# Moving an aggregation and a spread of sums ahead of a product in a graph network's layers: one TensorE order, one VectorE order

## The reference

```python
for l in range(attn_w.shape[0]):                       # 3 layers
    si = x @ attn_w[l, :d]
    sj = x @ attn_w[l, d:]
    scores = si[:, :, None] + sj[:, None, :] + attn_b[l]
    scores = jnp.where(scores >= 0, scores, 0.2 * scores)
    scores = jnp.where(mask, scores, -jnp.inf)
    attn = jax.nn.softmax(scores, axis=-1)
    agg = jnp.einsum('bij,bjd->bid', attn, x)
    h = layernorm(x + agg, g1[l], beta1[l])
    ff = jax.nn.gelu(h @ W1[l] + b1[l], approximate=False) @ W2[l] + b2[l]
    x = layernorm(h + ff, g2[l], beta2[l])
```

## Time and profile before

| | |
|---|---|
| median of 3 runs | 1641.13 us (1639.92 to 1642.3) |
| the profiled execution, its own time | 1641.3 us |
| its span, first to last instruction | 1639.5 us |
| mean granted PE clock, share of full | 0.996 |
| busy share of the span: PE, PEld | 98%, 88% |
| busy share: DVE, ACT, POOL | 81%, 75%, 81% |

### The profile page before, as it was taken

One profiled execution on the slowest core, in us unless ns is written; L12 is line 12 of the kernel. 1 busy time (PEld: TensorE's weight loads), 2 busy tenths in 40 slices (PEclk: granted clock), 3 DMA queues, 4 the chain that ended last, 5 costly groups with the idle time before them and its releaser, 6 DMA issues.

```text
span 1639.5 us, 40121 instructions
## 1 busy us (share of the span) xinstructions
PE 1611.0 (98%) x12036; PEld 1435.8 (88%) x12036; DVE 1320.2 (81%) x5321; ACT 1232.7 (75%) x2856; POOL 1327.4 (81%) x2367
## 2 busy tenths in 40 slices
PE   9999999978999999999999999999999999999997
PEld 8888888867898999989899898989989899898986
DVE  5999999987777777787877777777787888888875
ACT  7888898866777676777767776677777778787874
POOL 7788888856677787877878777787878999999996
PEclk9999999999999999999999999999999999999999
DMA  6334322212122121212213121121211222222211
GB/s 229 104 104 140 101 91 91 90 40 91 40 101 91 50 77 38 77 50 66 77 40 102 64 77 63 52 77 39 77 42 61 77 77 77 77 90 85 82 47 57
DMA packets 141721, 127.62 MB, mean 78 GB/s; under 512 B 12240, under 2 KB 132560, under 8 KB 141648
## 3 DMA queue, kind: packets, MB, share of 16 engines
q1 hardware_dynamic: 141648, 126.81, 24.2%
HBM read 89.04 MB, written 37.75 MB: 77 GB/s over the span
## 4 chain that ended last, share of the span: by engine, by line
PE 75%; DVE 1%; POOL 1%; ACT 0%; issue 0%; POOLq 0%; DVEq 0%; ACTq 0%
PE ps L45 33%; PE ps L979 32%; PE ps L951 5%; PE ps L965 3%; PE ps L943 1%; PE ps L958 1%; POOL n L169 0%; DVE gnn_junk L1111 0%; DVE xo L1222 0%; DVE res L1154 0%; POOL gnn_inv_last L913 0%; ACT gnn_w_hi L1067 0%; DVE gnn_st L1225 0%; DVE gnn_st L1178 0%; DVE gnn_st L1159 0%
## 5 line engine op out<-in xcount | busy, mean ns | idle before, releaser
L979 PE MATMUL ps<-gnn_w_hi,gnn_g_hi 128*128 128x256 f32 x1536 | 434.0, 283 | 1.5 <-DVE gnn_res L1174 1.5
L979 PE MATMUL ps<-gnn_w_lo,gnn_g_hi 128*128 128x256 f32 x1536 | 429.0, 279 | 0.0
L979 PE MATMUL ps<-gnn_w_hi,gnn_g_lo 128*128 128x256 f32 x1536 | 428.7, 279 | 0.0
L1079 ACT ACTIVATE gnn_g_hi<-ps,b_cols 128x512 fp32r<-128x512 f32 x384 | 264.4, 688 | 199.3 <-PE ps L45 199.3
L1182 DVE TENSOR_TENSOR gnn_g_lo<-ps,gnn_g_hi 128x512 fp32r<-128x512 f32 x384 | 262.8, 684 | 103.5 <-ACT ps L1080 103.4
L45 PE MATMUL ps<-gnn_hT_hi,gnn_w_hi 128*128 128x512 f32 x768 | 337.9, 440 | 0.0
L45 PE MATMUL ps<-gnn_hT_lo,gnn_w_hi 128*128 128x512 f32 x768 | 303.6, 395 | 0.0
L45 PE MATMUL ps<-gnn_hT_hi,gnn_w_lo 128*128 128x512 f32 x768 | 303.5, 395 | 0.0
L979 PEld LDWEIGHTS ps<-gnn_w_hi,gnn_g_hi 128*128 128x128 f32 x1536 | 288.7, 188 | 3.9 <-DVE gnn_res L1174 1.7
L979 PEld LDWEIGHTS ps<-gnn_w_lo,gnn_g_hi 128*128 128x128 f32 x1536 | 288.8, 188 | 2.3
L979 PEld LDWEIGHTS ps<-gnn_w_hi,gnn_g_lo 128*128 128x128 f32 x1536 | 288.7, 188 | 0.0
(11 more groups left out here) (145 smaller groups left out, 3994.4 us busy)
## 6 DMA issues: line engine op xcount, KB each, us to landing
x<-hist SPq DMA_DIRECT2D x49, 512.0 KB, 3.9
hist<-xo SPq DMA_DIRECT2D x48, 512.0 KB, 3.9
aw<-in_L_gnn_attn_w SPq DMA_DIRECT2D x48, 256.0 KB, 4.1
gmask<-mask_hist SPq DMA_DIRECT2D x48, 256.0 KB, 4.1
att_xT_raw<-in_xT SPq DMA_DIRECT2D x16, 512.0 KB, 3.3
att_xl<-in_x SPq DMA_DIRECT2D x16, 512.0 KB, 3.5
gnn_fin<-hist SPq DMA_DIRECT2D x15, 512.0 KB, 3.9
out<-gnn_fin SPq DMA_DIRECT2D x15, 512.0 KB, 3.0
```

Source lines behind the costliest of these rows:

```text
L979: mm = e.matmul(FF2[j % 2], g[a][:, m, j * N:(j + 1) * N], W2[b][:, m, :], start=(n == 0), stop=(n == len(terms) - 1))
L1079: e.activation(g[0][:, m, :], FF1[FFB[m]], ACT.Gelu, bias=bias)
```

## The change

Two tables of places are altered, one on PE and one on DVE. No instruction is added or taken out. On PE aggregation 3 moves from behind product 4 to behind product 3, and the spread of the sums from behind product 5 to the same place. On DVE `residual1` of graph 2 goes from behind low part 2 to behind low part 3, that of graph 3 from low part 3 to low part 4. `stats1` of graph 2 goes from low part 3 to low part 4, that of graph 3 from low part 4 to low part 5, and `mean_variance1` with it, so that it stands directly ahead of `masked_sums`.

```diff
                         if more >= 1:
-                            for j in {0: (0, 1), 3: (2,), 4: (3,)}.get(m, ()):
+                            for j in {0: (0, 1), 3: (2, 3)}.get(m, ()):
                                 aggregate(t1, p1, j)
-                        if more >= 2 and m == 5:
+                        if more >= 2 and m == 3:
                             spread_sj(t + 2)
...
-                        if more >= 1 and m < GROUP:
-                            residual1(t1, p1, m)
-                        if more >= 1 and 1 <= m <= GROUP:
-                            stats1(t1, m - 1)
-                        if more >= 1 and m == GROUP:
+                        if more >= 1 and m in (0, 1, 3, 4):
+                            residual1(t1, p1, (0, 1, 1, 2, 3)[m])
+                        if more >= 1 and m in (1, 2, 4, 5):
+                            stats1(t1, (0, 0, 1, 1, 2, 3)[m])
+                        if more >= 1 and m == 5:
                             mean_variance1(t1)
```

## The result

| | before | after |
|---|---|---|
| median | 1641.39 us | 1682.44 us (1681.16 to 1682.92) |
| ratio, 95% interval | | 1.0249 (1.0236 to 1.0262) |
| span of the profiled execution | 1639.5 us | 1679.4 us |
| mean granted PE clock | 0.996 | 0.997 |

The change makes the kernel 41.05 us slower. The forecast was 1683 us, in a range of 1674 to 1697.

A forecast was written before the change was run, and what follows sets the result against it. PE's own list was taken to bound the layers, with almost no slack behind low part 7; PE's moves cost 0, new waits 22.8 + 19.4 = 42 us, so 1641.3 + 42 gives 1683 us, range 1674 to 1697.

The forecast's parts named there:

- The bound: In the layers PE never waits; low part 7 has 0 or 0.07 us slack before PE's second product takes the eighth piece.
- PE's own cost at 0: Moving aggregation 3 and the spread on PE saves or costs nothing itself; two aggregations together take 0.87 us, one 0.43.
- The chain: DVE's list from low part 4 to low part 7 takes 5.23 us without idle time, starting low part 7 0.95 us later.
- The wait: PE waits for low part 7 in the second product: 0.95 us in 24 steps, 0.88 in 22, 42 us together.
- The upper bound: A 0.19 us weight load exposed behind each PE wait (9 us), or whole recorded instruction lengths (13 us): 1692 to 1696 us.
- The price by distances: DVE's instructions priced from start to start; whole recorded lengths would add 0.28 us a step, about 1696 us.
- What was costed at nothing: Aggregation 3's wait for graph 1's residual (cover 0.12 us), SP's load for a later step (cover 0.8), POOL's late normalization.
- Faster by saved returns: PE's saved returns are worth 0.19 us each and DVE makes up the rest: 1624 us, chance 0.03.
- no change: Low part 7 is late but PE does not mind, or the shifts go faster: 1641 us, chance 0.03.
- a second wait: Aggregation 3 waits for graph 1's residual, or the first sum for its load: 9 us more, 1692 us, chance 0.08.
- a fallen clock: Each new PE wait brings a slow-clock stretch costing 1.6 us a step: 75 us, 1758 us, chance 0.02.
- What I named as signs: About 46 PE waits of L979 for L1182, 40 us total; DVE never idle between low parts 4 and 7; 26.8 us steps.

The follow-up runs named there:

- the PE half: Kernel before with only the new PE table (aggregation 3 and the spread behind product 3), DVE's list as before: 1643.71 us against 1641.49, ratio 1.0013.

## Why the prediction was right, point by point

- *The bound.* PE's list, with no slack behind low part 7, was right: one instruction of 0.33 us ahead of it cost 15 us in 46 steps, 13.6 of them at low part 7, and the same one behind low part 4 nothing.
- *PE's own cost at 0.* Right: 1.31 us for the block that stands together, 0.87 + 0.44 before; the PE half alone lost 2 us, and that by a delay of low part 7 of some 0.06 us.
- *The chain.* 5.23 us were forecast from low part 4 to low part 7; measured are 1073.59 - 1068.39 = 5.20. Low part 7 was to be 0.95 us late; it is 0.92. The difference lies in low parts 5 and 6, priced at 0.62 us; when DVE has not stood idle ahead of them the next instruction follows after 0.59 (1069.93 to 1070.52) and 0.61.
- *The wait.* 0.95 and 0.88 us a step were forecast, 42 us in all. From start to start it is 0.92 us in most of the 24 steps without slack and 0.85 in the 22 others, 41.2 us in all: low part 7 is 0.92 late in both, less the slack of 0 and 0.07. So the slack was read rightly, and what the forecast has too much is the 0.03 us of the chain. The upper bound with a weight load of 0.19 us exposed behind each wait did not come: the second distance is longer by about 0.1 us, but the first has grown by correspondingly less, so nothing comes on top of what low part 7 is late.
- *The price by distances.* By whole recorded lengths the time would have been 1696 us. It came out at 1682, and the rows of after show followers 0.59 to 0.61 after the start of a record of 0.68 or 0.69. The distances in the trace decide. The Trainium skill, page "VectorE: DVE Perf Modes", section "The DRAIN you can't avoid", which I had cited for whole lengths, adds that a next instruction that is not held starts earlier; these rows agree with that addition.
- *What was costed at nothing.* Aggregation 3 made no wait. The load of x made none in the changed kernel, and the run with the shifts moved showed how near it was. POOL was not late for PE, but the place where its work falls beside DVE's sums, which I had not priced, went with 12 us in another run.
- *The rivals.* Faster by saved returns, no change, a second wait, a fallen clock: none came. The granted clock in the layers is 1.00, as before.
- *What I named as signs.* The 46 waits of L979 for L1182 and the full DVE between low parts 4 and 7 are there, and nearly all steps are 26.7 to 26.9 us long. "40 us in total" was wrong for PE's list (29.5), as matmuls' records cover part of each wait; the distances give 41.

## What to carry to other kernels

Where the bounding engine never waits, look for the awaited result that arrives with the least to spare, and follow the list of the engine that makes it back to the last place where that engine stood idle; only work added behind that place costs, and in this kernel it cost one for one, less what the result had to spare. Two moves that use the same idle time cannot both have it, so price them as one. A reordering on one engine also moves where two other engines' work falls side by side, and that can cost time of its own.

## What the runs showed of the hardware that I had not expected

- DVE's attention sums (L1111) take 0.42 us alone and 0.95 beside POOL's products (L858), and how many are slow went with which of them started first: with POOL's start 0.6 us earlier against DVE's sums, four instead of two were slow, and the transposes on PE came 0.6 us later in each of 24 steps.
- After a wait of PE the weights' load and its matmul are recorded at the same time, and the second matmul follows after 0.23 us instead of 0.12 or 0.15. That is no cost beyond the awaited result's delay: the two distances together grow by what the result is late, less its slack (0.84 + 0.08 us for 0.92). The load came 0.05 us after the end of the awaited record in each of the 46 steps.
- The list of PE's waits shows 29.5 us and that of its weight loads 38.7 where the starts show 41.2, since the record of the matmul or load ahead of a wait covers a part of it.
